# An encoder block with experts on one core: ranks of two sequences at a time, pad rows written once in front of the loop, and last tiles that overlap

## The reference

```python
h = tdnn(x, W, b, gamma, beta)            # windows, matmul, relu, batch norm
h = h + attention(layernorm(h))           # 8 heads of 16, a bias per key column
xf = layernorm(h)                         # 3872 rows
logits = xf @ Wr + br                     # 8 experts
e = argmax(logits)                        # top 1, its gate is softmax of one = 1
out = h + relu(xf @ W1[e] + b1[e]) @ W2[e] + b2[e]
```

## Time and profile before

| | |
|---|---|
| median of 3 runs | 352.64 us (348.5 to 356.53) |
| profiled execution | 345.34 us, span of its trace 343.6 us |
| busy PE, DVE, ACT, POOL | 80%, 66%, 66%, 62% of the span |
| HBM read, written | 10.69 MB, 8.44 MB |
| granted TensorE clock, mean | 0.916 |

### The profile page before, as it was taken

How to read it: one execution, slowest core, us unless ns; L and a number is a source line. 1 busy time by engine, 2 the same in 40 slices (tenths; PEclk the granted TensorE clock), 3 DMA queues, 4 the chain that set the end, 5 groups by cost and what they waited for, 6 DMA issues and landing times. The chain is left out here.

```text
span 343.6 us, 7885 instructions
## 1 busy us (share of the span) xinstructions
PE 275.7 (80%) x2139; PEld 215.0 (63%) x2139; DVE 225.4 (66%) x714; ACT 227.0 (66%) x843; POOL 213.2 (62%) x299
## 2 busy tenths in 40 slices
PE   3890969899999998897898879856008999999980
PEld 2660746556767665665656656545007999999970
DVE  2895676888988999877787686455403565656540
ACT  3851378889888998697897788640005777777740
POOL 7044554787766867888888886667721454545551
PEclk9995698999999999999999999895557999999996
DMA  3200990000000000001000100112634333333300
GB/s 94 79 2 1 303 281 18 0 2 1 3 0 2 1 3 15 16 15 32 15 24 23 31 15 17 30 31 73 171 98 122 93 101 109 94 104 108 91 13 0
DMA packets 15579, 19.15 MB, mean 56 GB/s; under 512 B 3960, under 2 KB 11676, under 8 KB 15537
## 3 DMA queue, kind: packets, MB, share of 16 engines
q1 hardware_dynamic: 11520, 11.73, 12.1%
q0 software_dynamic: 3296, 5.98, 6.0%
q10 hardware_dynamic: 720, 0.94, 0.9%
HBM read 10.69 MB, written 8.44 MB: 56 GB/s over the span
## 5 line engine op out<-in xcount | busy, mean ns | idle before, releaser
L467 ACT ACTIVATE P<-psS,nmax 121x121 f32<-121x121 f32 x256 | 88.9, 380 | 17.9 <-DVE nmax L709 17.2
L929 PE MATMUL psS<-patT,qT 128*121 128x484 f32 x128 | 64.3, 607 | 2.5 <-ACT P L467 1.7
L396 POOL DMA_INDIRECT out<-y_out,xg x38 | 36.9, 971 | 46.9 <-issue 31.5
L362 POOL TENSOR_TENSOR P<-P,rden 121x968 f32<-121x968 f32 x31 | 56.5, 1823 | 8.2 <-DVE rden L781 7.6
L467 ACT ACTIVATION_READ_ACCUMULATOR P<-psS,nmax 121x1 f32 x256 | 57.4, 224 | 0.0
L835 DVE TENSOR_SCALAR hT<-psT,b1T 128x128 f32<-128x128 f32 x76 | 23.3, 347 | 46.7 <-PE psT L1062 46.6
L709 DVE TENSOR_REDUCE nmax<-psS 121x4 f32<-121x484 f32 x64 | 41.5, 651 | 15.0 <-PE psS L929 15.0
L941 PE MATMUL psT<-ident,P 121*121 121x121 f32 x256 | 34.4, 277 | 15.2 <-POOL P L362 13.2
L941 PEld LDWEIGHTS psT<-ident,P 121*121 121x121 f32 x256 | 29.7, 185 | 21.9 <-POOL P L362 19.2
L374 POOL DMA_INDIRECT region_d<-rows,pos x32 | 34.9, 1091 | 8.8 <-issue 8.8
L476 ACT ACTIVATE PT<-psT 121x968 f32<-121x968 f32 x32 | 32.0, 1000 | 12.6 <-PE psT L941 12.6
(11 more groups left out here) (210 smaller groups left out, 620.4 us busy)
## 6 DMA issues: line engine op xcount, KB each, us to landing
xg<-region_d SPq DMA_DIRECT2D x38, 128.5 KB
W_sb<-in_L_ffn_W SPq DMA_DIRECT2D x1, 2048.0 KB, 9.2
region_d<-pads SPq DMA_DIRECT2D x11, 128.5 KB, 4.3
out<-y_out,xg POOLq DMA_INDIRECT x38
region_d<-pads ACTq DMA_DIRECT2D x4, 128.5 KB
b_bc<-in_L_ffn_b SPq DMA_DIRECT2D x1, 512.0 KB, 5.9
region_d<-rows,pos POOLq DMA_INDIRECT x32
xs<-in_x ACTq DMA_DIRECT2D x1, 402.5 KB, 3.9
```

The costliest lines, as they stand in the source:

```text
L362: pool.tensor_tensor(P[0:L, i % 2, :, :], P[0:L, i % 2, :, :], rden[0:L, i % 2, :].unsqueeze(2).to_broadcast([L, H, L]), ALU.mult).then_in ...
L396: pool.indirect_dma_start(out, bass.IndirectOffsetOnAxis(xg[:, u, 2 * D:ROW].bitcast(I32), 0), y_out[:, u, :], None, bounds_check=N - 1, o ...
L467: ins = act.activation(P[0:L, t % 2, h, :], psS[0:L, h // HG, h % HG * L:(h % HG + 1) * L], ACT.Exp, bias=nmax[0:L, h:h + 1], accum_out=de ...
L929: pe.matmul(psS[0:L, g, 0:HG * L], qT[:, t // 2 % 2, g, t % 2 * L:t % 2 * L + L], kbd[:, t % 4, g, :], start=True, stop=True).then_inc(s_S, 1)
```

## The change

The groups are now sixteen of two sequences, and a group's ranks and places come in step b0 + nb + 8 in place of b0 + nb + 10. `expert_onehot` moves one step ahead and behind the `bn_aggr` of its step. Scatters in the loop begin at step 11 in place of 16, and 8 follow the loop in place of 13.

Pad rows are no longer written behind the rows of each expert. Two transfers write pads to the first 128 rows of every expert and to the seven spare tiles, where the seven transfers stood, and POOL waits for both (`d_pads` 32) ahead of `norm1(0)`. The last tile of an expert now begins early enough to end at its last row, so it repeats rows of the tile in front; DVE works out which rows are repeated (`again`, `mask`) and gives POOL indices `sidx` in which these rows are out of bounds. The number of tiles stays 38.

```diff
-GROUPS = tuple((b, 4) for b in range(0, B - 4, 4)) + ((B - 4, 2), (B - 2, 2))
+GROUPS = tuple((b, 2) for b in range(0, B, 2))
...
-        def write_pads(eng, experts):
-
-            eng.wait_ge(s_pads, 2)
-            eng.wait_ge(r_start, 1)
-            for e in experts:
-                first = eng.value_load(pad_row[0:1, e:e + 1], min_val=e * CAP, max_val=e * CAP + N)
-                eng.dma_start(region_d[bass.ds(first, 128), :], pads[:, :]).then_inc(d_pads, 16)
...
             sp.wait_ge(s_pads, 2)
-            for n in range(XT):
-                sp.dma_start(region_d[E * CAP + n * 128:E * CAP + (n + 1) * 128, :], pads[:, :]).then_inc(d_extra, 16)
-
-            write_pads(sp, range(0, E // 2))
+            sp.dma_start(region_d[0:E * CAP, :].rearrange("(e r) c -> r e c", r=CAP)[0:128, :, :],
+                         pads[:, :].unsqueeze(1).to_broadcast([128, E, ROW])).then_inc(d_pads, 16)
+            sp.dma_start(region_d[E * CAP:E * CAP + XT * 128, :].rearrange("(n r) c -> r n c", r=128),
+                         pads[:, :].unsqueeze(1).to_broadcast([128, XT, ROW])).then_inc(d_pads, 16)
 
             sp.wait_ge(d_rows, 16 * B)
-            sp.wait_ge(d_pads, 16 * E)
-            sp.wait_ge(d_extra, 16 * XT)
+            sp.wait_ge(d_pads, 32)
             sp.wait_ge(r_row, 1)
...
+            pool.wait_ge(s_rowid, 1)
+            pool.wait_ge(d_pads, 32)
             pool.wait_ge(l_rows, 16 * N_ROWS)
             norm1(0)
...
-                if t >= 16 and t < B + 3:
-                    scatter_rows(t - 16)
-            for b in range(B - 13, B):
+                if t >= 11 and t < B + 3:
+                    scatter_rows(t - 11)
+            for b in range(B - 8, B):
                 scatter_rows(b)
 
             for s in range(NT):
                 u = s % RING
+                pool.wait_ge(f_si, s + 1)
                 pool.wait_ge(f_y, s + 1)
-                pool.indirect_dma_start(out, bass.IndirectOffsetOnAxis(xg[:, u, 2 * D:ROW].bitcast(I32), 0), y_out[:, u, :], None,
+                pool.indirect_dma_start(out, bass.IndirectOffsetOnAxis(sidx[:, s:s + 1], 0), y_out[:, u, :], None,
                                         bounds_check=N - 1, oob_is_err=False).then_inc(f_sca[u], 16)
...
-            write_pads(act, range(E // 2, E))
...
-                    if t - 4 in group_at:
-                        row_places(group_at[t - 4], 1 - par)
+                    if t - 2 in group_at:
+                        row_places(group_at[t - 2], 1 - par)
...
                 if t - 1 in group_at:
                     expert_rank(group_at[t - 1])
                 if t - 2 in group_at:
-                    expert_onehot(group_at[t - 2])
-                if t - 3 in group_at:
-                    expert_seen(group_at[t - 3])
+                    expert_seen(group_at[t - 2])
                 if has(t, 3):
                     dve.wait_ge(s_st, b + 1)
                     dve.bn_aggr(mv2[0:L, b % 2, :], st2[0:L, :]).then_inc(s_ag, 1)
+                if t - 1 in group_at:
+                    expert_onehot(group_at[t - 1])
                 if rows_first:
...
-            dve.tensor_copy(pad_row[0:1, :], psU[0:1, E:2 * E]).then_inc(r_start, 1)
             ne, tiles, skip = (cnt[0:1, n, :] for n in range(3))
-            rlink(dve.tensor_copy(ne, psU[0:1, 0:E]))
-            rlink(dve.tensor_tensor(cmpt[0:1, :, :], ne.unsqueeze(2).to_broadcast([1, E, B - 1]),
-                                    tile_starts[0:1, :].unsqueeze(1).to_broadcast([1, E, B - 1]), ALU.is_gt))
-            rlink(dve.tensor_reduce(tiles, cmpt[0:1, :, :], AX.X, ALU.add))
+            dve.tensor_copy(ne, psU[0:1, 0:E]).then_inc(r_chain, 1)
+            rl[0] += 1
+            dve.tensor_scalar(dlim[0:1, 0, :], psU[0:1, 0:E], -128.0, 0.0, ALU.add, ALU.max).then_inc(r_chain, 1)
+            rl[0] += 1
+            dve.wait_ge(r_chain, 1)
+            dve.tensor_tensor(cmpt[0:1, :, :], ne.unsqueeze(2).to_broadcast([1, E, B - 1]),
+                              tile_starts[0:1, :].unsqueeze(1).to_broadcast([1, E, B - 1]), ALU.is_gt).then_inc(r_chain, 1)
+            rl[0] += 1
+            dve.wait_ge(r_chain, 2)
+            rlink(dve.tensor_tensor(lim[0:1, 0:E], dlim[0:1, 0, :], base_e[0:1, :], ALU.add))
+            dve.tensor_reduce(tiles, cmpt[0:1, :, :], AX.X, ALU.add).then_inc(r_chain, 1)
+            rl[0] += 1
+            rlink(dve.tensor_tensor(dlim[0:1, 1, :], lim[0:1, 1:E + 1], lim[0:1, 0:E], ALU.subtract))
...
+            dve.tensor_tensor(past[0:1, 2, :, :], past[0:1, 0, :, :], dlim[0:1, 1, :].unsqueeze(1).to_broadcast([1, NT, E]),
+                              ALU.mult).then_inc(r_chain, 1)
+            rl[0] += 1
+            dve.wait_ge(r_chain, rl[0])
+            rlink(dve.tensor_reduce(tab[0:1, 1:3, :], past[0:1, 1:3, :, :], AX.X, ALU.add))
+            rlink(dve.tensor_tensor(tab[0:1, 3, :], tab[0:1, 1, :], tile_rows[0:1, :], ALU.add))
+            dve.scalar_tensor_tensor(out=row0[0:1, :], in0=tab[0:1, 2, :], scalar=lim[0:1, 0:1], in1=tab[0:1, 3, :],
+                                     op0=ALU.add, op1=ALU.min).then_inc(r_row, 1)
+            dve.wait_ge(r_row, 1)
+            dve.tensor_tensor(again[0:1, :], tab[0:1, 3, :], row0[0:1, :], ALU.subtract).then_inc(r_again, 1)
+            dve.wait_ge(r_mask, 1)
+            rlink(dve.tensor_scalar(mask[:, :], psO[:, 0:NT], part0[:, 0:1], float(NOROW), ALU.is_gt, ALU.mult))
...
+                dve.tensor_tensor(sidx[:, s:s + 1], xg[:, u, 2 * D:ROW].bitcast(I32), mask[:, s:s + 1], ALU.bitwise_or).then_inc(f_si, 1)
...
-            rank_at = {b0 + nb + 10: g for g, (b0, nb) in enumerate(GROUPS)}
+            rank_at = {b0 + nb + 8: g for g, (b0, nb) in enumerate(GROUPS)}
 
             pe.wait_ge(l_rows, 16 * N_ROWS)
-            pe.wait_ge(s_colio, 3)
+            pe.wait_ge(s_colio, 6)
...
-            pe.matmul(psU[0:1, 0:E], ones_bf[0:L, 0:1], seen[0:L, NG, :], start=True, stop=True)
-            pe.matmul(psU[0:1, E:2 * E], ones_bf[0:L, 0:1], seen[0:L, NG, :], start=True, stop=False)
-            pe.matmul(psU[0:1, E:2 * E], ones_bf[0:1, 0:1], base_row[0:1, 0, :], start=False, stop=True).then_inc(r_cnt, 1)
...
-            pe.wait_ge(r_start, 1)
-            pe.wait_ge(r_chain, 1)
+            pe.wait_ge(r_chain, 2)
+            pe.wait_ge(r_again, 1)
+            pe.matmul(psO[:, 0:NT], ones_bf[0:1, :], again[0:1, :], start=True, stop=True).then_inc(r_mask, 1)
```

More of the change, by code:

```diff
@@ L172, in build @@
         tscan = sb("tscan", [1, E])
-        pad_row = sb("pad_row", [1, E], I32)
-        past = sb("past", [1, 2, NT, E])
-        tab = sb("tab", [1, 2, NT])
+        base_e = sb("base_e", [1, E])
+        lim = sb("lim", [1, E + 1])
+        dlim = sb("dlim", [1, 2, E])
+        past = sb("past", [1, 3, NT, E])
+        tab = sb("tab", [1, 4, NT])
         eid = sb("eid", [1, NT], I32)
         row0 = sb("row0", [1, NT], I32)
+        again = sb("again", [1, NT], BF16)
+        part0 = sb("part0", [128, 1])
+        mask = sb("mask", [128, NT], I32)
+        sidx = sb("sidx", [128, NT], I32)
         xg = sb("xg", [128, RING, ROW])
@@ L209, in build @@
         s_top = sem("s_top")
-        r_oh, r_sum, r_seen, r_rank, r_pick, r_pos, r_cnt, r_start, r_chain, r_eid, r_row = map(
-            sem, "r_oh r_sum r_seen r_rank r_pick r_pos r_cnt r_start r_chain r_eid r_row".split())
-        d_rows, d_pads, d_extra = sem("d_rows"), sem("d_pads"), sem("d_extra")
+        r_oh, r_sum, r_seen, r_rank, r_pick, r_pos, r_cnt, r_chain, r_eid, r_row, r_again, r_mask, f_si = map(
+            sem, "r_oh r_sum r_seen r_rank r_pick r_pos r_cnt r_chain r_eid r_row r_again r_mask f_si".split())
+        d_rows, d_pads = sem("d_rows"), sem("d_pads")
         s_pads, s_rowid = sem("s_pads"), sem("s_rowid")
@@ L323, in _ @@
             pool.iota(base_row[:, :, :], pattern=[[0, 4], [CAP, E]], base=0, channel_multiplier=0, **fl).then_inc(s_colio, 1)
+            pool.iota(part0[:, :], pattern=[[0, 1]], base=0, channel_multiplier=1, **fl).then_inc(s_colio, 1)
             pool.memset(seen[:, 0, :], 0.0).then_inc(s_colio, 1)
+            pool.iota(base_e[:, :], pattern=[[CAP, E]], base=0, channel_multiplier=0, **fl).then_inc(s_colio, 1)
+            pool.memset(lim[:, E:E + 1], float(E * CAP + XT * 128)).then_inc(s_colio, 1)
             pool.memset(pads[:, 0:2 * D], 0.0).then_inc(s_pads, 1)
@@ L737, in logits @@
                         dve.wait_ge(s_R2, q + 1)
-                        dve.tensor_tensor(lg[0:L, q % 2 * 2:q % 2 * 2 + 2, :] if q < NP - 2 else lg[0:L, 0:2, :],
+                        dve.tensor_tensor(lg[0:L, 0:2, :],
                                           psB[0:L, 1 - par, 0:2 * E].rearrange("p (k e) -> p k e", k=2),
@@ L810, in _ @@
             rl[0] += 1
-            rlink(dve.tensor_tensor(past[0:1, 1, :, :], past[0:1, 0, :, :], skip.unsqueeze(1).to_broadcast([1, NT, E]), ALU.mult))
```

(15 more changed lines are left out.)

## The result

The changed kernel takes 373.25 us (median of 4 runs, 372.26 to 376.54), the kernel before beside it 350.57 us. The ratio is 1.069, with a 95% interval of 1.056 to 1.081. It is slower by 22.7 us, where 26 were forecast. The profiled execution took 372.26 us with a span of 370.2; the sum of the prediction for it was 371.5. A ratio compares executions in the fast state alone, so it can differ by up to a per cent from the quotient of two medians.

What follows compares the result with a forecast made beforehand. It took a ring of engines waiting for one another, with PE full only in the experts, as the bound. Profiled 345.34 + 25.6 + 2.4 + 5.6 - 7.4 = 371.5 us; median 352.64 + 26.2 = 378.8, say 379; range 367 to 389.

Steps and rivals of the forecast that it cites:

- The start: Ahead of the loop: POOL's wait for both pad writes starts `norm1(0)` at 58.1 in place of 32.46, +25.6 us.
- rival 3: Pad writes striped over eight places go at half the rate, +5.3 us, 384 us; chance 0.04.
- Scatters in the loop: Steps 11 to 15: five more scatters at 0.48 us each, +2.4 us.
- Ranks in groups of two: Loop steps from 8: 54 added DVE instructions at 0.105 us each, +5.6 us.
- Rival 1: The ring doesn't feel the rank work in the loop: 373 us; chance 0.17.
- rival 2: Loop dearer: instructions at full 0.17 us, +3.6, and PE's low clock, 5 us; 388 us; chance 0.14.
- The passage: Loop's end to first tile: 8 scatters follow in place of 13, gate from 255.79 to 248.4, -7.4 us.
- The table and the experts: DVE's table ends at 246.3, 2 us under the gate; the experts, still 38 tiles, cost 0.
- The time: Whole kernel: profiled execution 371.5 us; median 352.64 + 26.2 = 378.8, say 379 us.
- rival 4: Not slower: the pad wait costs at most 12.1 us, time up to 359.7 us; chance 0.03.

Runs made afterwards that it cites:

- the pads moved: Changed kernel with both pad writes issued ahead of SP's wait for `attr`, POOL's wait left ahead of `norm1(0)`: 349.77 us, 1.011 of before.
- more pads: Changed kernel with a third write of pads, 1.05 MB, between the two and the wait raised to 48: 380.17 us, one execution.
- the kernel with groups of two alone: Kernel before with only its groups changed, to sixteen of two: 353.48 us, 1.024 of before.
- the kernel before with a filled loop: Kernel before with one unread 384-column matmul on PE in each even step from 6 to 30: 349.92 us, 1.004 of before.
- the kernel with the late wait: Changed kernel with POOL's waits for pads and row numbers moved from ahead of `norm1(0)` to the first scatter, step 11: 348.44 us, 1.010 of before.
- filling the passage: Late-wait kernel with groups of four, scatters from step 13, plus unread PE matmuls from step 32 and ahead of the first tile: 348.97 us, 1.000 of before.
- the kernel with groups of four: Late-wait kernel with seven groups of four and two of two, scatters from step 13, 10 behind the loop: 348.83 us, 1.000 of before.

## Why the prediction was right, point by point

**The start: right, +24.7 for +25.6.** The mechanism was shown three times: the wait moved (gone), the pads moved (gone), more pads (longer). Within it two terms were off and in part cancelled. The rate: the added 1.05 MB cost 3.4 to 3.65 us, not 5.3. I had read the rate from windows in which the last of seven small writes ran out, and took their thin end for the rate. The end of the data before: I took 52.3, it was 53.1. The half microsecond from the data to the landing was right (56.6 to 57.06). So 52.3 + 5.3 + 0.5 made 58.1, and 53.1 + 3.4 + 0.5 is 57.0. For these bytes the slope of the Trainium skill's fit ("DMA: Bandwidth & Descriptors", Anatomy of one DMA), which is for GpSimd's path, gives an estimate of 2.4 us. The measurement, 3.4 to 3.65, decides, and it lies between that estimate and mine.

**Stripes (rival 3): didn't come.** 288 GB/s for blocks 4,473,856 bytes apart is more than the 198 that I read for the contiguous ones. By the rule on row pitch in the Trainium skill ("DMA: Bandwidth & Descriptors", Latency and other measured facts) this pitch is not slowed, and the run agrees.

**Scatters in the loop: right in the price of a steady one, too dear by 1 us in all.** 0.47 us each by quiet steps, 0.48 forecast, but the five together cost 1.4 us and not 2.4. The step that was mis-sized is that five of them cost five times the steady price where they begin.

**Ranks in groups of two: right in kind, too dear by 1.4 to 2 us.** 0.33 to 0.39 for two steps (from 8 to 10 it is 11.46 against 11.07), not 0.47. The step that was mis-sized is the price for an instruction: I averaged 0.09 and 0.12 of the earlier trace rows, the runs show 0.07 to 0.08. That they work on half as many numbers may be why; this was not tested. The new place of `expert_onehot` is not it, for the kernel with groups of two alone, where it stayed, has the same 0.33. Rival 1 is refuted by the same kernel.

**What the loop had beside.** Two long steps of 1.0 us each were rival 2's clock, at two of its five us. Its other half, instructions at their full 0.17, is refuted. The first four steps took 22.10 us in place of 22.95, and that is no gain of the change: the step from 1 to 2 took 4.73 us in the profile of before and 3.88 in that of the kernel before with a filled loop, whose program is the same up to there. So the +6.8 are, step range by step range, -0.85 from this chance, +1.4 for the scatters, +2.0 for the long steps and some +4.2 for the rank work, and that 6.8 came so close to 8.0 is in part luck: the long steps stood in no term of the sum.

**The passage: -5.2 for -7.4.** The five scatters less were worth 6.6 as forecast, and the gate comes 3.11 us behind the last one's start, before 4.70, another 1.6 (I had 0.8). The step that failed is the silent one: that the first scatter behind the loop keeps its distance from the loop's end. From the last reciprocal to it are 14.16 us (255.59 to 269.75), before 11.17 (to 235.24). In the kernel with the late wait, the same instructions take 12.11 (232.21 to 244.32):

```profile
224.07 0.20 DVE L781 RECIPROCAL rden<-den 121x8 f32<-121x8 f32 x1 [0.68 <-ACT P L467]
```

```profile
244.32 1.02 POOL L374 DMA_INDIRECT region_d<-rows,pos  x1 [0.31 <-issue]
```

What differs in the windows is the clock. In the changed kernel it is at 0.50 from 260 on:

```profile
255.00:260.00 5.00, 2.95 (x34) 0.85 0.09 25
260.00:265.00 5.00, 3.85 (x35) 0.50 0.09 25
```

In the kernel with the late wait, whose last reciprocal is at 232.21, it holds to 240:

```profile
235.00:240.00 5.00, 3.75 (x54) 1.00 0.09 25
```

The low clock comes with the longer way in all twelve profiles. In the three in which the clock held for 6 us behind the last reciprocal (before, groups of two alone, late wait) the way is 11.2 to 12.1 us; in the nine in which it was low by then it is 13.5 to 16.4. One of the nine is the kernel before with a filled loop (14.06), whose passage is that of the kernel before, so a way of 14 us is not a price of the change. But the attempt to set the clock by filling the passage came too late in it to test that, so this cause is likely and not shown, and why the clock falls sooner in some executions is open.

**The table and the experts: right.** The table ended 0.9 us under the gate; I had 2 us; it began later, as the whole passage did. `sidx` cost nothing that can be read (+0.3 us).

**The time.** 379 was forecast for the median, 373 came; the sum for the profiled execution was 371.5 and it took 372.26. The difference lies in the step from the one to the other: I added the 7.3 us by which the profiled run of before was under its median. That run was faster than all four timed ones of a kernel whose runs spread by 2.4%, and the changed kernel's runs spread by 1.1% and lie close to its profile.

That 371.5 and 372.26 lie so close is luck in part. The start was 0.9 and the loop 1.2 us too dear in the sum, the passage had 2.2 too much gain, and these nearly cancel. In rival 4, the 12.1 us that the wait might have cost leave out the 5.6 of the rank work; with them it is 6.5, which makes that rival less likely still.

## What to carry to other kernels

What this wait cost came neither from its place nor from its transfer, but from what stood in the queue ahead of the transfer: 4 MB of weights stood between a cheap wait and cheap bytes, and either one moved gave 25 us back. Put a wait where its data is first needed, or issue what is waited for first. In this ring of engines each small instruction cost a fraction of its length (0.07 of 0.17 us), and halving a group's size doubles them. Where PE's waits in a loop make the granted clock fall now and then, a matmul that nobody reads, short enough to end within the wait, can pay for itself: it gave about 1% in the loop with groups of four and nothing in the kernel before. And a profile of one execution holds chances of its own, here 0.85 us in one early step and 3 us in the passage; a term that is read from it should be looked for in a second one.

## What the runs showed of the hardware

SP was held for 11.0 to 11.8 us at the issue of a 16 KB load, in all twelve profiles, while 4 MB of weights issued ahead of it in pieces of 512 and 2048 bytes were moved; the same queue then issued 1 MB of pads in 0.42 us.

The granted clock fell to 0.50 in single steps of a loop in which PE was busy about 90% of the time (113.6 of 125 us in the kernel with groups of four), behind waits for POOL of 1.3 to 1.6 us (in the profiles of the changed kernel and of the one with groups of four), and one fill of 0.81 us every two steps kept it at 1.00. Waits of 1.27 us (at 145 in the kernel before) and of 1.89 us (at 121 in the one with groups of four) stand in front of steps at the full clock, so their length alone does not tell which step will be a long one. The Trainium skill ("TensorE: Matmul & The Clock Gate", A second HAM failure mode: psum-queue depth-cycling) tells of a kernel whose PE idles briefly and often between groups of matmuls and goes back and forth between the two levels; these windows agree. Removing it was worth 1.0, 1.4 and 3.1 us for the three pairs of steps that had it in this kernel.

A first tile at the full clock was worth nothing over one at half (0.50 from 264 to 266 in the kernel with groups of four; 87.0 us for the experts both ways), which I had not expected.
